# Early-fusion transformer block on one core: thresholds guessed from exponential sums, the third count's signs reused, VectorE's chains split

## The reference

```python
h = concat([layernorm(patches @ W + b, cls, + pos) * gamma + beta, txt])      # 64 x 165 x 256
xn = layernorm(h)
q, k, v = split(xn @ W_qkv.T + b_qkv)                # 16 heads of 16
scores = q @ k.T * 256 ** -0.5                       # 64 x 16 x 165 x 165
keep, for each of the 165 rows of a head, the 49 largest scores; the others become -inf
h = h + softmax(kept) @ v @ W_out.T + b_out
h = h + moe(layernorm(h))    # shared expert of width 192, 64 routed experts, 8 a token, at most 128 slots each
```

## Time and profile before

| | |
|---|---|
| median of 3 runs | 3900.95 us (3892.15 to 3911.05) |
| profiled execution | 3892.95 us, span of the profile 3891.2 us |
| busy, share of the span | DVE 3269.3 us (84%), ACT 3206.1 (82%), PE 2844.4 (73%), POOL 2168.0 (56%) |
| chain that ended last | DVE 59%, issue 14%, ACT 14%, PE 6%, DMA 4% |
| main loop, from 200 to 3420 us | DVE about 94% busy, ACT about 93% |
| routed experts, from 3460 us | DVE 105 us and ACT 57 us busy in 432 us |

### The profile page before, as it was taken

One profiled execution on the slowest core, in us unless ns is written; L12 is line 12 of the kernel. 1 busy time (PEld: TensorE's weight loads), 2 busy tenths in 40 slices (PEclk: granted clock), 3 DMA queues, 4 the chain that ended last, 5 costly groups with the idle time before them and its releaser, 6 DMA issues.

```text
span 3891.2 us, 94555 instructions
## 1 busy us (share of the span) xinstructions
PE 2844.4 (73%) x21253; PEld 2306.8 (59%) x21253; DVE 3269.3 (84%) x14277; ACT 3206.1 (82%) x14721; POOL 2168.0 (56%) x2919
## 2 busy tenths in 40 slices
PE   4677777777777777777777777777777777763776
PEld 3566566656666656666666666666666666553554
DVE  1999999999999999999999999999999999961222
ACT  4999999999999999999999999999999999930111
POOL 2235556565556566565555565555556565555554
PEclk7788988898888898888888888888888888877999
DMA  1000100110100110101110101110101110004776
GB/s 46 10 18 16 18 14 17 19 19 16 18 14 18 19 19 17 18 14 18 18 19 16 19 14 18 18 19 16 18 14 18 19 19 16 11 10 104 174 172 138
DMA packets 212430, 118.62 MB, mean 30 GB/s; under 512 B 108528, under 2 KB 209476, under 8 KB 211812
## 3 DMA queue, kind: packets, MB, share of 16 engines
q1 hardware_dynamic: 166692, 91.53, 8.8%
q0 software_dynamic: 45120, 20.49, 5.9%
HBM read 66.51 MB, written 33.38 MB: 26 GB/s over the span
## 4 chain that ended last, share of the span: by engine, by line
DVE 59%; issue 14%; ACT 14%; PE 6%; DMA 4%; DVEq 2%; POOL 2%; SPq 0%; POOLq 0%; ACTq 0%
DVE X L876 9%; ACT JK L687 9%; DVE X L867 7%; DVE M L873 7%; DVE PR L944 7%; DVE S L849 7%; DVE M L879 4%; DVE RD L949 3%; DMA E<-x_rows,IX 2%; PE bank L1373 2%; ACT E L669 1%; ACT E L673 1%; POOL slot_token L546 1%; DMA out<-E,IX 1%; PE bank L1378 1%
## 5 line engine op out<-in xcount | busy, mean ns | idle before, releaser
L546 POOL DMA_INDIRECT slot_token<-TOKI,SLOT x1024 | 1341.7, 1310 | 308.6 <-issue 272.3
L687 ACT ACTIVATE JK<-S,thr 128x165 f32<-128x165 f32 x2688 | 1120.8, 427 | 39.9 <-POOL thr L510 39.7
L687 ACT ACTIVATE JK<-S,t 128x165 f32<-128x165 f32 x1344 | 562.4, 433 | 0.1
L687 ACT ACTIVATION_READ_ACCUMULATOR JK<-S,thr 128x1 f32 x2688 | 524.2, 195 | 0.0
L867 DVE SCALAR_TENSOR_TENSOR X<-S,t 128x165 f32<-128x165 f32 x1344 | 509.3, 379 | 10.5 <-POOL t L522 6.8
L849 DVE TENSOR_SCALAR_CACHE_REDUCE S<-bank 128x165 f32<-128x165 f32 x1344 | 362.1, 321 | 160.4 <-ACT JK L687 65.5
L1226 PE MATMUL bank<-IDENT,PR 128*128 128x128 f32 x1344 | 367.3, 306 | 170.8 <-ACT PTI L697 143.8
L673 ACT ACTIVATE E<-bank,nb 128x165 f32<-128x165 f32 x1344 | 438.2, 397 | 14.6
L873 DVE MAX8 M<-X 128x8 f32<-128x165 f32 x1344 | 433.5, 323 | 0.0
L879 DVE MAX8 M<-X 128x8 f32<-128x165 f32 x1344 | 424.2, 320 | 0.0
L876 DVE MATCH_REPLACE8 X<-M,X 128x165 f32<-128x165 f32 x1344 | 420.6, 313 | 0.0
(11 more groups left out here) (174 smaller groups left out, 7043.9 us busy)
## 6 DMA issues: line engine op xcount, KB each, us to landing
slot_token<-TOKI,SLOT POOLq DMA_INDIRECT x1024
S<-in_w_gate SPq DMA_DIRECT2D x64, 192.0 KB, 2.8
S<-in_w_up SPq DMA_DIRECT2D x64, 192.0 KB, 3.1
S<-in_w_down SPq DMA_DIRECT2D x64, 192.0 KB, 3.8
x_rows<-X SPq DMA_DIRECT2D x64, 160.0 KB
H<-in_txt SPq DMA_DIRECT2D x64, 128.0 KB, 2.1
QA<-QT SPq DMA_DIRECT2D x512, 10.3 KB
QB<-QT SPq DMA_DIRECT2D x512, 10.3 KB
```

The costliest lines, as they stand in the source:

```text
L546: pool.indirect_dma_start(slot_token, bass.IndirectOffsetOnAxis(SLOT[r % 2][0:n, c, k:k + 1], 0), TOKI[r % 2][0:n, c:c + 1], None, bounds_ ...
L687: act.activation(JK[:, t % 8, :], S[r % 2][:, t, :], ACT.Sign, bias=(t0, t1, t2[r % 2])[n][:, t:t + 1], scale=-1.0, accum_out=(c0, c1, c2) ...
```

## The change

There are three edits, and with them new orders on all engines.

The Abs pass goes. The Exp pass now also sums its row (sz, sum of exp((s - mx)/16)), and the first threshold is a product of polynomials of sz and mx, five small operations on GpSimd where there was one. nb is a step of its own (`maxima`), which ScalarE does ahead of other work.

The third count writes its signs to BELOW, six tiles long, instead of to a scratch tile, and `pick` forms X for three tiles at once as (BELOW > 0) * S. So `pick` now waits for the third count of its group, and the count of group g waits until the product of group g-2 is done.

VectorE's chains are cut into steps that stand between other steps; the fallback works on three tiles at a time. The flag is formed (`doubt`) some instructions ahead of the register load.

```diff
 GUESS, SLOPE = 0.85, 0.0165          ->  (-3.823, 4.0717 / T, 1.2576 / 16, 3.0789 / 16 / T), 0.0205
@@ GpSimd, guess
-                pool.tensor_scalar(t0[:, lo:hi], sa[r % 2][:, lo:hi], GUESS / T, 1.0, ALU.mult, ALU.mult)\
-                    .then_inc(s_up, 1)
+                pool.tensor_scalar(v0[:, lo:hi], mx[:, lo:hi], GUESS[3], GUESS[1], ALU.mult, ALU.add).then_inc(s_up, 1)
+                pool.tensor_scalar(v1[:, lo:hi], mx[:, lo:hi], GUESS[2], GUESS[0], ALU.mult, ALU.add).then_inc(s_up, 1)
...
+                pool.tensor_tensor(v0[:, lo:hi], v0[:, lo:hi], sz[:, lo:hi], ALU.mult).then_inc(s_up, 1)
...
+                pool.tensor_tensor(v0[:, lo:hi], v0[:, lo:hi], v1[:, lo:hi], ALU.add).then_inc(s_up, 1)
...
+                pool.tensor_tensor(t0[:, lo:hi], v0[:, lo:hi], mx[:, lo:hi], ALU.mult).then_inc(s_up, 1)
@@ ScalarE, exps and the third count
-                    act.activation(E[r % 2][:, t, :], chunks(bS[g % 3], GROUP, T)[:, t % GROUP, :], ACT.Abs,
-                                   accum_out=sa[r % 2][:, t:t + 1]).then_inc(s_exp, 1)
...
                     act.activation(E[r % 2][:, t, :], chunks(bS[g % 3], GROUP, T)[:, t % GROUP, :], ACT.Exp,
-                                   bias=nb[:, t:t + 1], scale=SCALE).then_inc(s_exp, 1)
+                                   bias=nb[:, t:t + 1], scale=SCALE, accum_out=sz[:, t:t + 1]).then_inc(s_exp, 1)
...
+            def below(i, r, g):
...
+                if g >= 2:
+                    act.wait_ge(s_pick, PK_N * i + issued(GROUP * (g - 2)) + 1)
+                for t in range(GROUP * g, GROUP * (g + 1)):
+                    act.activation(BELOW[:, t % (2 * GROUP), :], S[r % 2][:, t, :], ACT.Sign, bias=t2[r % 2][:, t:t + 1],
+                                   scale=-1.0, accum_out=c2[:, t:t + 1]).then_inc(s_cnt, 1)
@@ VectorE, pick
-                    dve.scalar_tensor_tensor(X[n % 5][:, :], S[r % 2][:, n, :], t2[r % 2][:, n:n + 1], S[r % 2][:, n, :],
-                                             ALU.is_lt, ALU.mult).then_inc(s_pick, 1)
+                if n < NT and n % GROUP == 0:
+                    g = n // GROUP
+                    at = n % (2 * GROUP)
+                    dve.wait_ge(s_cnt, CN * i + 2 * NT + n + GROUP)
+                    dve.scalar_tensor_tensor(X[g % 3][:, :, :], BELOW[:, at:at + GROUP, :], 0.0, S[r % 2][:, n:n + GROUP, :],
+                                             ALU.is_gt, ALU.mult).then_inc(s_pick, 1)
@@ SyncE, iteration (load_patch stood first; both halves of diagonal, store_out, store_x, load_text followed)
+                if has(i + 1):
+                    diagonal(i + 1, 0)
+                if has(i - 3):
+                    store_x(i - 3, (r - 3) % RING)
+                if has(i + 1):
+                    diagonal(i + 1, 1)
```

More of the change, by code:

```diff
@@ L718, in iteration @@
             def iteration(i, r):
+                if has(i - 1):
+                    below(i - 1, (r - 1) % RING, 0)
                 if has(i):
+                    maxima(i, 0)
                     exps(i, r, 0)
                 if has(i - 1):
-                    count(i - 1, (r - 1) % RING, 2, range(0, 3))
+                    below(i - 1, (r - 1) % RING, 1)
                 if has(i):
+                    maxima(i, 1)
                     exps(i, r, 1)
                 if has(i - 1):
-                    count(i - 1, (r - 1) % RING, 2, range(3, 6))
+                    below(i - 1, (r - 1) % RING, 2)
                 if has(i - 3):
@@ L729, in iteration @@
                 if has(i):
-                    exps(i, r, 2)
+                    maxima(i, 2)
                 if has(i - 2):
                     transposed(i - 2, 0)
-                if has(i - 1):
-                    count(i - 1, (r - 1) % RING, 2, range(6, 9))
-                    count(i - 1, (r - 1) % RING, 2, range(9, 12))
+                if has(i):
+                    exps(i, r, 2)
                 if has(i - 3):
@@ L763, in iteration @@
                     front_k(i + 1)
+                if has(i):
+                    maxima(i, 6)
+                    exps(i, r, 6)
                 if has(i - 2):
@@ L767, in iteration @@
                     count(i, r, 0, range(0, AHEAD))
-                    exps(i, r, 6)
-                    count(i, r, 0, range(AHEAD, NT))
                 if has(i + 1):
@@ L772, in iteration @@
                 if has(i):
+                    count(i, r, 0, range(AHEAD, NT))
                     count(i, r, 1, range(0, AHEAD))
@@ L1098, in iteration @@
                 if has(i - 1):
+                    pick(i - 1, (r - 1) % RING, 15)
+                if has(i - 3):
+                    back_top3(i - 3)
+                    back_weights(i - 3)
+                if has(i - 1):
+                    pick(i - 1, (r - 1) % RING, 16)
+                if has(i - 3):
+                    back_weights2(i - 3, (r - 3) % RING)
+                    back_place(i - 3)
+                    back_place2(i - 3)
+                    back_place3(i - 3)
+                if has(i - 1):
+                    pick(i - 1, (r - 1) % RING, 17)
+                if has(i - 3):
+                    back_slots(i - 3)
+                if has(i - 1):
+                    rank(i - 1)
+                if has(i - 3):
+                    back_slots2(i - 3, (r - 3) % RING)
+                if has(i - 1):
+                    pick(i - 1, (r - 1) % RING, 18)
+                    pick(i - 1, (r - 1) % RING, 19)
                     pick(i - 1, (r - 1) % RING, 20)
@@ L1308, in iteration @@
                     transposes(i - 2, 0)
+                if has(i):
+                    scores(i, 3)
                 if has(i - 3):
@@ L1327, in iteration @@
                     front_qk(i + 1, 0)
+                if has(i - 3):
+                    back_down(i - 3)
                 if has(i - 2):
@@ L1330, in iteration @@
                 if has(i - 3):
-                    back_down(i - 3)
                     back_route(i - 3)
+                if has(i):
+                    scores(i, 6)
                 if has(i - 2):
@@ L1349, in iteration @@
                     back_proj(i - 2)
-                if has(i + 1):
-                    scores(i + 1, 1)
-                    scores(i + 1, 2)
                 if has(i - 1):
@@ L1356, in iteration @@
                     front_embed(i + 2, (r + 2) % RING)
+                if has(i + 1):
+                    scores(i + 1, 1)
+                    scores(i + 1, 2)
             batches(pe, iteration)
```

366 lines of the change are left out of this document (201 added, 165 removed).

## The result

The kernel after takes 3629.45 us (median of 4 runs, 3623.73 to 3633.12), before 3900.17 (4 runs, 3892.15 to 3911.05): a ratio of 0.9303, 95% interval 0.9284 to 0.9323, 271 us less. The forecast was 3670. The profiled execution has a span of 3631.4 us (3891.2 before) and TensorE's mean granted clock is 0.915 (0.857 before).

What follows compares the result with a forecast made beforehand. VectorE's own instructions and sequencer were taken to bound the loop; 2.1 + 1.05 + 0.7 - 0.3 = 3.55 us an iteration, times 64 = 227 us, gave 3670 us, range 3595 to 3800.

Steps and rivals of the forecast that it cites:

- VectorE alone bounds the loop: Steady loop: VectorE waits for no other engine; its own instructions and sequencer set the 53.15 us an iteration.
- cover: ScalarE without Abs: 49.3 becomes 45.4 us an iteration, worth nothing by itself, but covering the new waits.
- The product, 2.1 us: VectorE's pick: seven wide products at 0.60 us replace 21 at 0.30, saving 2.1 us an iteration.
- Chains split, 1.05 us: VectorE: gaps before instructions that need the one just before vanish, 1.05 us an iteration; bounds 0.6 and 1.2.
- The flag early, 0.7 us: VectorE's iteration start: sequencer running ahead covers most of the flag's wait, 0.7 us saved, from 0 to 1.2.
- A new wait for the sums, 0.3 us: VectorE before PO: waits for TensorE's routing sums over MK, costing 0.3 us an iteration, from 0 to 1.2.
- The sum: Whole iteration: 2.1 + 1.05 + 0.7 - 0.3 = 3.55 us saved, a period of 49.6.
- Rival A: VectorE loses its lead, ScalarE or GpSimd feeding it late at one place: some 3800 us; chance 0.18.
- B: Each of seven wide products waits for its own ScalarE counts, 0.68 us each: slower, 3973 us; chance 0.08.
- C: The guessed threshold misses and the fallback runs, 90 us a batch, slower from three batches on; chance 0.03.
- D: Jump over the longer fallback body costs 3.4 us like the jump back: no change, 3883 us; chance 0.05.

Runs made afterwards that it cites:

- The chain kernel: Kernel after with VectorE's split chains put together again, the flag still seven instructions ahead of its load: 3809.67 us, ratio 0.9766.
- three narrow products: Kernel after with each group's wide product formed as three 165-element instructions, scalar a constant 0.0: 3679.22 us, ratio 0.9437.
- the third chip: Four variants of the kernel after (loop of eight, third threshold earlier, place later, all together): 3905.99, 3995.29, 3833.8, 3822.2 us; before took 4047.2 there.
- column of zeros: Three 165-element products a group, but the scalar 0.0 read from an SBUF column instead of being a constant: 3773.18 us, ratio 0.9674.

## Why the prediction was right, and where its terms were off

*VectorE alone bounds the loop.* Right, and shown from both sides: 3.8 us less for ScalarE in the kernel before gave nothing, and 6.2 us more in the kernel after took the bound away from VectorE, at 363 us. The prediction had the removed pass as cover, and that is what it is; how much of the gain the 3.8 us that were really taken away protect was not measured.

*The product, 2.1 us.* It measured 2.18, but less than half of it for the reason that I gave. The wide one costs 0.578 (0.60 forecast). The step "0.30 is its cost in a full row", taken as the price of a narrow product, mixed two things: 0.24 us for 165 elements and 0.06 for the scalar read from SBUF. By the rule of the Trainium skill ("VectorE: DVE Perf Modes", section on the TRN2 errata) the narrow and the wide product would be an estimated 0.232 and 0.576 us; the traces have 0.240 and 0.578, where the scalar is a constant. The rule has no term for a scalar from SBUF, which is why it missed the old product. The 0.8 us that the prediction worked out from it are near the 1.0 of the width alone. That the forecast of 2.1 came true is in that sense luck: the old price was measured, but what made it was not the width alone.

*Chains split, 1.05 us.* This term failed in its size: 2.8 us were measured, 1.13 in gaps and 1.65 in the instructions themselves. The gaps were counted rightly from the profile's idle column. Missed was that an instruction whose neighbour waits for it also loses its overlap with it, and the profile shows that in no idle column, only in the distance between starts. The chain kernel shows both halves, 1.3 and 1.8. Its 180 us also hold some 0.8 us an iteration of waiting for TensorE's scores.

*The flag early, 0.7 us.* At the start of an iteration the idle time fell by 0.58 us (0.49 on average over eleven turns). The reason given, "if the sequencer runs ahead while they execute, most of the wait is covered", is what its records show: 0.7 us of the load and the jump lie under the masks and aggregations, and the wait ahead of the aggregation holds it, as said. What the term lacked is that load and jump themselves would take longer. From the load's start to the first instruction it was 1.1 us at the end in the earlier trace rows and is 1.3 to 1.5 at three of four ends now; with three narrow products it is 1.0 at two ends, and there 0.2 to 0.3 us of idle time stay. In the new order the early flag is worth 1.0 us.

*A new wait for the sums, 0.3 us.* In the kernel after it is hardly there (5 times, 2.8 us), and a collision of 0.61 us with GpSimd, which I did not have, stands in its place. Without the collision the wait is 0.34. Not forecast either are 0.49 us of small gaps before `take` and before back_norm's X.

Of the Trainium skill's "SBUF — State Buffer" (the section on two separate sides) a rule bears on that: VectorE and GpSimd share a port pair that one of them holds for a whole instruction. The row agrees in that the pair takes 1.02 us beside two GpSimd instructions of 0.73 and 0.40 without them, and ends 0.05 us behind the second of them. Which port it is, no run here shows.

*The sum.* 2.18 + 2.78 + 0.58 - 0.61 - 0.49 = 4.44 us against 3.55: the excess is the overlap of the chains, less what the collision and the small gaps took. That the total came within 41 us of the forecast is in part luck: 1.7 us that the chains gave beyond their term stand against 1.1 that the collision and the small gaps took, neither of which was in the sum. Rival A (3800) and B (3973) did not happen: three waits of 448 products. C did not: no fallback line. D did not in its size: 0.8 us at an iteration's end, 4 only at the jump back; but the jump over the fallback costs 0.3 us more at three of the four ends than before. Rival A in a form that I did not have, TensorE feeding late, is what the third chip shows.

## What to carry to other kernels

Read the cost of a small instruction from start to start, and count for a dependent neighbour both the gap and the lost overlap; splitting chains of small instructions gave more here than the wider product. A pass on an engine with slack can be worth nothing when removed, and much once the bound engine has been shortened below it: remove both together, and test with the pass put back. An experiment that adds or drops instructions also moves everything behind them: compare the waits and the jump, too, before a time is taken as the price of the edit. When a kernel is near two bounds, time it on more than one chip.

## What the runs showed of the hardware

- A scalar read per partition from SBUF makes a scalar_tensor_tensor of 128x165 cost 0.30 us instead of 0.24 from start to start (kernels with three products, column of zeros and constant).
- Two 128x64 tensor_scalars beside GpSimd's tensor_tensors of 128x256 took 1.02 us instead of 0.40.
- VectorE's sequencer loads the flag and starts the jump while three masks execute (flag load from 1978.04, last mask until 1978.91). A taken jump over the fallback costs 0.20 to 0.22 us or 0.52 to 0.54, by its place in the loop; the loop's jump back leaves 4.0 to 4.7 us of idle time in the kernel after, and in a loop of eight iterations it comes once in eight.
- The same kernel of before took 3896.8 and 3897.0 us on two chips and 4047.2 on a third.
